# Attention scores and weighted sums as plain fp32 matmuls on half arrays, in double steps

## The reference, cut to what matters

```python
q, k, v = x @ Wq, x @ Wk, x @ Wv          # H = 16 heads, HKV = 4 key heads, D = 64
q, k = rope(q), rope(k)
scores = einsum('bkgqd,bkpd->bkgqp', q, k) * D ** -0.5
scores = where(causal, scores, -1e30)
out = einsum('bkgqp,bkpd->bkgqd', softmax(scores), v) @ Wo
```

## Time and profile before

| | |
|---|---|
| Median of 3 runs | 4915.38 us (4910.9 to 4915.8) |
| Span of the profiled execution | 4914.1 us |
| Its granted TensorE clock, mean | 0.959 |
| Attention's loop, about | 1770 to 3575 us of the span |

### The profile page before, as it was taken

The page is one execution under the profiler, slowest core; times in us unless marked ns, Lnnn a source line. Parts: engine busy times, 40 slices in busy tenths (PEclk is TensorE's granted clock), DMA queues, the critical chain, the costliest instruction groups (busy, mean ns, idle before and its releaser), DMA issues. The chain is left out here.

```text
span 4914.1 us, 82249 instructions
## 1 busy us (share of the span) xinstructions
PE 4375.7 (89%) x20280; PEld 3077.8 (63%) x20311; DVE 3433.2 (70%) x7334; ACT 2814.4 (57%) x6629; POOL 1757.2 (36%) x1411
## 2 busy tenths in 40 slices
PE   7888888789999979999999999999966549999996
PEld 3333333356666568888888888888855437777775
DVE  7999999934434878888888888888844443333336
ACT  7777777522221068888888888888833224444441
POOL 5989989700100021212121221212135553333330
PEclk8999999999999989999999999999987769999999
DMA  1000000021102530202112021202044425554548
GB/s 44 13 13 13 13 27 9 9 87 57 47 17 82 178 102 26 53 26 52 42 44 53 26 52 28 58 26 53 26 155 143 143 97 155 155 157 152 157 138 344
DMA packets 305965, 377.40 MB, mean 77 GB/s; under 512 B 123200, under 2 KB 236608, under 8 KB 300240
## 3 DMA queue, kind: packets, MB, share of 16 engines
q1 hardware_dynamic: 232784, 257.37, 17.3%
q0 software_dynamic: 26112, 73.44, 4.2%
q10 hardware_dynamic: 46944, 45.16, 3.4%
HBM read 223.07 MB, written 152.76 MB: 76 GB/s over the span
## 5 line engine op out<-in xcount | busy, mean ns | idle before, releaser
L1739 DVE TENSOR_TENSOR probsT<-ps_t,probsT 128x512 fp32r<-128x512 f32 (+3 forms) x1280 | 779.5, 609 | 137.8 <-ACT probsT L1679 116.2
L1679 ACT ACTIVATE probsT<-ps_t 128x512 fp32r<-128x512 f32 (+3 forms) x1280 | 686.6, 536 | 256.1 <-PE ps_t L1527 231.3
L1671 ACT ACTIVATE probs<-ps_s,negm 128x512 f32<-128x512 f32 (+3 forms) x1297 | 812.5, 627 | 28.1 <-DVE negm L1732 27.1
L1539 PE MATMUL ps_o<-probsT,vbuf 128*128 128x512 f32 (+3 forms) x2560 | 815.8, 402 | 6.8 <-ACT folding L1685 6.3
L1514 PE MATMUL ps_s<-kbuf,qbuf 128*128 (+1 forms) x2602 | 768.7, 380 | 57.8 <-ACT probs L1671 31.5
L1719 DVE TENSOR_REDUCE pmax<-ps_s 128x1 f32<-128x512 f32 (+3 forms) x1301 | 777.6, 600 | 47.3 <-PE ps_s L1514 23.0
L1527 PE MATMUL ps_t<-idn,probs 128*128 128x128 f32 x4352 | 694.8, 275 | 13.8 <-DVE probsT L1739 13.8
L527 POOL TENSOR_TENSOR dBx<-u,b_all 128x1024 f32<-128x1024 f32 x255 | 612.4, 2414 | 96.5 <-DVE h L623 66.8
L1527 PEld LDWEIGHTS ps_t<-idn,probs 128*128 128x128 f32 x4352 | 517.3, 141 | 135.3 <-DVE probsT L1739 40.9
L1514 PEld LDWEIGHTS ps_s<-kbuf,qbuf 128*128 128x128 f32 x2602 | 445.3, 189 | 177.9 <-issue 63.9
L1622 POOL CAST qbuf<-room_a 128x512 fp32r<-128x512 f32 x132 | 83.1, 630 | 1264.6 <-DMA room_a<-q_scr 754.1
(11 more groups left out here) (275 smaller groups left out, 6982.7 us busy)
## 6 DMA issues: line engine op xcount, KB each, us to landing
room_b<-xs ACTq DMA_DIRECT2D x294, 136.0 KB
room_a<-q_scr SPq DMA_DIRECT2D x528, 64.0 KB
room_c<-y SPq DMA_DIRECT2D x32, 1024.0 KB, 8.2
room_a<-W_guT SPq DMA_DIRECT2D x64, 384.0 KB
q_scr<-rot SPq DMA_DIRECT2D x64, 256.0 KB, 2.9
attn<-ostage SPq DMA_DIRECT2D x128, 128.0 KB
at<-attn SPq DMA_DIRECT2D x32, 512.0 KB
room_a<-W_downT SPq DMA_DIRECT2D x64, 192.0 KB
```

Source lines behind the costliest of these rows:

```text
L1539: last = nc.tensor.matmul(ps_o[:, lo:], vbuf[:, kb, :, :], probsT[:, g % SLOTS, part, lo:], start=kb == 0 and part == 0, stop=kb == BAND * ...
L1671: nc.scalar.activation(probs[:, k, at:at + n, :], ps_s[:, u % RING, 0:n * P], ACT.Exp, bias=negm[:, tile, :], accum_out=sums[:, s, j, c:c ...
L1679: nc.scalar.activation(probsT[:, g % SLOTS, 0, lo:], ps_t[:, t % 2, lo:], ACT.Copy).then_inc(high_t.sem, 1)
L1739: nc.vector.tensor_tensor(probsT[:, g % SLOTS, 1, lo:], ps_t[:, t % 2, lo:], probsT[:, g % SLOTS, 0, lo:].bitcast(F32), ALU.subtract).then ...
```

## The change

The split in high and low parts goes. Scores become one plain fp32 matmul over 64 rows; even and odd chunks use the lower and the upper 64 rows of the array (`rows`), where `qbuf` and `kbuf` hold the same data twice. Weighted sums become one plain fp32 matmul with 64 columns: even key blocks write the lower, odd ones the upper 64 rows of `ps_o`, and the fold adds them as before. The mask is added by two bf16 matmuls over 64 rows each. The turned groups are copied once, by ACT for even and by DVE for odd groups. `kbuf` is one buffer instead of two and is rewritten by quarters between two groups of heads, and `vbuf` comes straight from the staging buffer. TensorE's loop takes two steps at a time.

```diff
-    SLOTS = 4
+    SLOTS = 5
     LEAD = STEPS
     AHEAD = LEAD - BAND
-    LAG = 2
     LATE = STEPS - 2
...
+    def by_act(g):
+        return g % 2 == 0
...
+        def taken(eng, hx, t):
+            if ACT_TAKES[t + 1] > ACT_TAKES[t]:
+                eng.wait_ge(act_out.sem, act_out.at(hx, ACT_TAKES[t + 1]))
+            else:
+                eng.wait_ge(dve_out.sem, dve_out.at(hx, DVE_TAKES[t + 1]))
+        def bank_free(eng, hx, t):
+            if t >= 2:
+                taken(eng, hx, t - 2)
+            else:
+                taken(eng, hx - 1, NU * TURNS + t - 2)
...
-            def scores(hx, kslot, k, v):
+            def scores(hx, k, v):
                 s, j, c = CHUNKS[k][v]
                 u = k * STEPS + v
                 w = blocks(s, j, c) * P
+                rows = slice(HD * (u % 2), HD * (u % 2 + 1))
                 pe.wait_ge(exp_done.sem, exp_done.at(hx, u - RING + 1))
-                for part in range(2):
-                    last = nc.tensor.matmul(ps_s[:, u % RING, 0:w], qbuf[:, BAND * s + j, :],
-                                            kbuf[:, bass.ds(kslot, 1), part, c * CW:c * CW + w],
-                                            start=part == 0, stop=part == 1 and c < s)
+                last = nc.tensor.matmul(ps_s[:, u % RING, 0:w], qbuf[rows, BAND * s + j, :],
+                                        kbuf[rows, c * CW:c * CW + w], start=True, stop=c < s)
                 if c == s:
-                    last = nc.tensor.matmul(ps_s[:, u % RING, w - P:w], idn_r[:, :], mask_r[:, :], start=False, stop=True)
+                    for part in range(2):
+                        last = nc.tensor.matmul(ps_s[:, u % RING, w - P:w], halves_b[rows, part, :], mask_b[rows, part, :],
+                                                start=False, stop=part == 1)
                 last.then_inc(s_done.sem, 1)
             def turn(hx, k, g):
                 s, kb = GROUPS[k][g]
                 t = use(k, g)
                 pe.wait_ge(exp_done.sem, exp_done.at(hx, band_end(k, s)))
-                pe.wait_ge(t_out.sem, t_out.at(hx, t - 1))
+                bank_free(pe, hx, t)
                 for j in range(max(0, kb - BAND * s), BAND):
                     last = nc.tensor.transpose(ps_t[:, t % 2, j * P:(j + 1) * P], probs[:, k, place(k, s, j, kb), :], idn[:, :])
                 last.then_inc(t_done.sem, 1)
...
             def weigh(hx, group, k, g):
                 s, kb = GROUPS[k][g]
                 lo = max(0, kb - BAND * s) * P
-                pe.wait_ge(t_out.sem, t_out.at(hx, use(k, g) + 1))
+                rows = slice(HD * (kb % 2), HD * (kb % 2 + 1))
+                taken(pe, hx, use(k, g))
                 if kb == 0:
                     pe.wait_ge(o_ev.sem, o_ev.at(hx, 2 * k + (s == UNITS[k][1])))
                 if kb % BAND == 0:
                     pe.wait_ge(v_set.sem, v_set.at(group, V_ORDER.index(kb // BAND) + 1))
-                for part in range(2):
-                    last = nc.tensor.matmul(ps_o[:, lo:], vbuf[:, kb, :, :],
-                                            probsT[:, g % SLOTS, part, lo:],
-                                            start=kb == 0 and part == 0, stop=kb == BAND * s + BAND - 1 and part == 1)
-                last.then_inc(pv_done.sem, 1)
+                if kb == 1 and lo:
+                    nc.tensor.matmul(ps_o[rows, 0:lo], nothing[:, :], probsT[:, g % SLOTS, lo:2 * lo], start=True, stop=False)
+                nc.tensor.matmul(ps_o[rows, lo:], vbuf[:, kb, :], probsT[:, g % SLOTS, lo:],
+                                 start=kb == 0 or kb == 1 and not lo, stop=kb >= BAND * s + BAND - 2).then_inc(pv_done.sem, 1)
...
             with pe.Fori(0, NHEADS) as hx:
                 group = pe.snap(hx // GROUP)
-                slot = pe.snap(group % 2)
-                slot_next = pe.snap(((hx + 1) // GROUP) % 2)
+                group_next = pe.snap((hx + 1) // GROUP)
                 for k in range(NU):
                     def next_scores(v):
                         heads, unit, number = chunk(k, v, LEAD)
                         if number == 0 and unit == 0:
                             pe.wait_ge(q_ready.sem, q_ready.at(hx + 1, 2))
-                            pe.wait_ge(k_ready.sem, (hx + 1) // GROUP + 1)
                         elif number == 0:
                             pe.wait_ge(q_ready.sem, q_ready.at(hx + heads, 4))
-                        scores(hx + heads, slot_next if heads else slot, unit, number)
-                    for v in range(STEPS):
-                        if 0 < v < LATE:
-                            next_scores(v)
+                        if heads and unit == 0 and number < BANDS:
+                            pe.wait_ge(k_ready.sem, k_ready.at(group_next, K_ORDER.index(number) + 1))
+                        scores(hx + heads, unit, number)
+                    for v in range(0, STEPS, 2):
                         turn(hx, k, v)
-                        if v >= LAG:
-                            weigh(hx, group, k, v - LAG)
                         if v == FOLD[k]:
                             fold(hx, k, 0)
+                        turn(hx, k, v + 1)
+                        if v:
+                            weigh(hx, group, k, v - 2)
+                            weigh(hx, group, k, v - 1)
+                        next_scores(v + 1)
+                        next_scores(v + 2)
                     weigh(hx, group, k, STEPS - 2)
-                    next_scores(LATE)
                     weigh(hx, group, k, STEPS - 1)
-                    for v in range(LATE + 1, STEPS + 1):
-                        next_scores(v)
                     fold(hx, k, 1)
...
-            def keys(g):
...
+            def set_keys(g, c):
+                nc.gpsimd.tensor_copy(kbuf[:, c * CW:(c + 1) * CW], kstage[:, c * CW:(c + 1) * CW]).then_inc(k_ready.sem, 1)
             def queries(hx, n):
-                j, low = QUEUE[n], slice(HD, P)
-                tiles = slice(BAND * j, BAND * (j + 1))
-                after(q_ld[j].sem, q_ld[j].at(hx))
-                nc.gpsimd.tensor_copy(qbuf[:, tiles, :], qstage[:, tiles, :]).then_inc(high_q.sem, 1)
-                after(high_q.sem, high_q.at(hx, n + 1))
-                nc.gpsimd.tensor_tensor(qbuf[low, tiles, :], qstage[low, tiles, :], qbuf[low, tiles, :].bitcast(F32),
-                                        ALU.subtract).then_inc(q_ready.sem, 1)
-                after(q_ready.sem, q_ready.at(hx, n + 1))
+                tiles = slice(BAND * QUEUE[n], BAND * (QUEUE[n] + 1))
+                after(q_ld[QUEUE[n]].sem, q_ld[QUEUE[n]].at(hx))
+                nc.gpsimd.tensor_copy(qbuf[:, tiles, :], qstage[:, tiles, :]).then_inc(q_ready.sem, 1)
             def set_values(g, n):
                 b = slice(BAND * V_ORDER[n], BAND * (V_ORDER[n] + 1))
-                nc.gpsimd.tensor_copy(vbuf[:, b, :, :], vnext[:, b, :, :].bitcast(F32)).then_inc(v_set.sem, 1)
+                nc.gpsimd.tensor_copy(vbuf[:, b, :], vstage[:, b, :]).then_inc(v_set.sem, 1)
...
+                with pool.Fori(0, GROUP - 1) as j4:
                     head_queries(pool.snap(g * GROUP + j4))
+                head = pool.snap(g * GROUP + GROUP - 1)
+                after(s_done.sem, s_done.at(head, STEPS))
+                for n in range(2):
+                    queries(head + 1, n)
+                after(k_ld.sem, k_ld.at(g + 1))
+                for c in K_ORDER:
+                    after(s_done.sem, s_done.at(head, K_USED[c]))
+                    set_keys(g + 1, c)
+                for n in range(2, BANDS):
+                    queries(head + 1, n)
...
...
-                        high(hx, k, v)
+                        if by_act(v):
+                            take_turned(hx, k, v)
...
-            def low(hx, k, g):
+            def take_turned(hx, k, g):
                 s, kb = GROUPS[k][g]
                 t, lo = use(k, g), max(0, kb - BAND * s) * P
-                dve.wait_ge(high_t.sem, high_t.at(hx, k * STEPS + g + 1))
-                nc.vector.tensor_tensor(probsT[:, g % SLOTS, 1, lo:], ps_t[:, t % 2, lo:],
-                                        probsT[:, g % SLOTS, 0, lo:].bitcast(F32), ALU.subtract).then_inc(t_out.sem, 1)
+                dve.wait_ge(t_done.sem, t_done.at(hx, k * STEPS + g + 1))
+                dve.wait_ge(pv_done.sem, pv_done.at(hx, k * STEPS + g - SLOTS + 1))
+                nc.vector.tensor_copy(probsT[:, g % SLOTS, lo:], ps_t[:, t % 2, lo:]).then_inc(dve_out.sem, 1)
```

More of the change, by code:

```diff
@@ L1341, in attention @@
     RING = 5
-    SLOTS = 4
+    SLOTS = 5
     LEAD = STEPS
     AHEAD = LEAD - BAND
-    LAG = 2
     LATE = STEPS - 2
+    K_USED = [max(k * STEPS + v + 1 for k in range(NU) for v, (s, j, chunk_no) in enumerate(CHUNKS[k]) if chunk_no == c) for c in range(BANDS)]
+    K_ORDER = sorted(range(BANDS), key=lambda c: K_USED[c])
     V_ORDER = sorted(range(BANDS), key=lambda b: max(k * STEPS + g for k in range(NU) for g, (s, kb) in enumerate(GROUPS[k]) if kb // BAND == b))
```

(52 more changed lines are left out.)

59 lines of the change are left out of this document (22 added, 37 removed).

## The result

The changed kernel takes 5686.15 us (median of 4 runs, 5682.56 to 5688.06) against 4915.59 for the kernel before beside it: ratio 1.157, 95% interval 1.155 to 1.159. It is 771 us slower. The forecast said slower, 5890 us, range 5330 to 6220. So direction and range held, but two of the steps behind the number were wrong, in opposite directions.

A forecast was written before the change was run, and what follows sets the result against it. The prediction took TensorE to bound the attention stage. Per head 15.7 + 12.0 + 1.6 + 0.3 + 1.7 - 0.8 = +30.5 us, times 32 is +976, on 4914 gives 5890 us; range 5330 to 6220.

The forecast's parts named there:

- Overlap: Scores and weighted sums on half arrays: a pair takes three periods, the halves overlapping only in part; +15.7 us per head.
- B-high stands behind A-low: TensorE's queue for a pair of half-array matmuls: program order holds B's first record back, so 1.29 us against 0.94.
- first rival: TensorE's half-array matmuls: halves overlap fully, changes of shape still cost; +14.2 us per head, about 5370 us; chance 0.27.
- Changes of shape: TensorE switching between full array, column halves and row halves: 60 per head at 0.20 us, +12.0 us per head.
- Masks: Masked score chunks, 16 per head: one fp32r matmul becomes two bf16 on 64 rows, 0.10 each, +1.6 us per head.
- Folds: End of a unit: the fold waits uncovered for ACT's copy, the next second turn for the normalising; +1.7 us per head.
- Relief: DVE, ACT and POOL lose copies and low parts: only TensorE's wait for ACT's exponentials goes, -0.8 us per head.
- None of it stands on the path: Work taken off DVE, ACT and POOL: it doesn't set the time, except TensorE's 0.8 us per head wait for exponentials.
- the period of 0.43 inside a pair: Sign for the forecast in score pairs: second record and partner's first start within some ns, the next 0.43 us later.
- four starts within two periods: Sign in a pair's records on TensorE that the partial overlap was wrong and the halves overlap.
- 0.09 stops: Sign for the forecast on TensorE: weight loads start 0.09 us after the previous matmul's columns ended, three times per double step.
- wrong altogether: Sign against the whole forecast: TensorE idle for ACT or for POOL's keys by more than 2 us per head.

The follow-up runs named there:

- e7: Kernel before the change, with DVE's low part of the turned groups cut to 16 columns: 4901.97 us, ratio 0.9975 to the kernel before.
- e9: As e2, but scores and weighted sums each two fp32r matmuls over the full array, the second with zeros: ratio 1.005 to the kernel before, head 56.98 us.
- e4: As e2, but score and mask matmuls take all 128 rows, the upper 64 rows of the queries zero: 5349.98 us, ratio 1.109 to the kernel before.
- e1: Changed kernel, with DVE's copy of a turned group ahead of the peak of the same step: 5212.82 us, ratio 1.081 to the kernel before.
- e2: As e1, with all four weighs of a unit's last double step ahead of its two score chunks: 5147.30 us, ratio 1.067 to the kernel before.

## Why the prediction was right, and where it was wrong

The reading of the kernel before held: TensorE bounds the stage, which e7 confirms against DVE, and all else follows from its queue. The forecast's time was 204 us too high. Step by step, per head, where +30.5 was forecast and +23.9 measured:

1. *Overlap: wrong.* The step that failed is "B-high stands behind A-low". The forecast gave +15.7; the halves overlap fully where both are ready, and by e9 the matmuls cost no more than before. The row that the first rival had on its side, L277 begun before its predecessor's columns had ended, could not settle it, since its two matmuls share rows of the array (112 and 128 of them). So no row of before spoke of two halves, and I took program order for a rule across them. That order does not hold across the halves. In the trace a pair of 256 and 128 columns starts its records at 0.00 (256), 0.01 (128), 0.17 (128) and 0.27 (256). The one at 0.17 is the fourth in the program, and it starts before the second, at 0.27. The rule of the Trainium skill that I had leaned on ("TensorE: Matmul & The Clock Gate", The mechanism: matmuls keep program order in start and in end) differs from this trace, and the measurement decides: here order holds within a part of the array only. The Trainium skill's "TensorEngine Tiling (Array Packing)", Key Properties (the parts operate independently), agrees with it.

2. *Changes of shape: right, mis-sized by a fifth.* 60 at 0.20 were forecast, +12.0. Measured are 0.14 to 0.19, by the gaps 20 x 0.143 + 20 x 0.194 + 20 x 0.15 = 9.7; by runs it is 0.15 each (e4) and 0.16 (e9). The 16-row shape of the first stage gave the stop (0.09) but its weight load has 128 columns, where the sums have 64.

3. *Masks: not measured by themselves.* e9, which has the second mask matmul too, lies 0.6 above before with all that it has, where +1.6 was forecast for the masks alone.

4. *Folds: right in kind, short in size.* +1.7 forecast. Idle before the folds is 2.9 in the changed kernel, of which 1.2 is DVE's late copy, so 1.7 was its own part (e1 shows 1.7 left). e2 won 1.94 with it, one change per unit included.

5. *Relief: wrong.* The step that failed is "None of it stands on the path". I took -0.8 and measured +12.0 (e1; 15.1 at the turns, less 3.1 that came back as late score pairs), since I had counted DVE's load and not its order. The change moved the scores to the end of a double step and left DVE's peak ahead of its copy. What is queued behind a waiting instruction I had worked out for the folds and for the keys, but not for this peak. It could be seen by laying DVE's loop beside TensorE's new one.

So the measured sum is 9.7 for the changes, 12.0 for DVE's order, 1.9 for the folds, and the 0.3 that is left for all the rest: 23.9. The forecast's +15.7 for a cost that is not there stood in for the +12.0 that I had overlooked. That two errors nearly cancelled is luck, and the range held the result for the wrong reason in part: the first rival (full overlap, 5370) described the matmuls and is off by the 12.0 x 32 = 383 us of DVE's order, less 9.7 against 12.0 for the changes. Of what was to show the forecast, the head of 85 to 89 us with TensorE over 90% busy and the period of 0.43 inside a pair failed, and the four starts within two periods, its own sign of full overlap, are what came. The 0.09 stops, three per double step, DVE and ACT under 60% and the wait for ACT's folding copy came true. Its sign for "wrong altogether" named idle time for ACT or POOL; the 10.3 us per head were for DVE, which no sign named.

One thing stays open: how much of the score pairs' lateness another order on ACT and DVE would win back. By the estimate under e2 it is 4 us per head at most, and the change would still be slower than before.

## What to carry to other kernels

Matmuls on different halves of the array ran at the same time at full rate, even with two plain fp32 records each, but only where the second was ready when the first began; and every change between full, row and column shape cost 0.14 to 0.19 us here; so count the changes per unit of work first, and use halves only where long runs of one shape can be made. When an engine's work is moved to the end of a longer step, walk through each other engine's program in order and ask what stands behind the instruction that now waits longest: an engine that is 47% busy cost half of this loss. A high busy share of TensorE hides a pair whose halves don't overlap: compare the starts of the records. Relief of an engine that doesn't bound the kernel is worth the bounding engine's idle time at most, which the rows show beforehand (1.6 us per head here, of which e7 won 0.4).

## What was not expected of the hardware

- Records of the two halves start 0.01 us apart although each plain fp32 matmul is two records, and a later matmul of one half starts before an earlier one of the other.
- The stop at a change of shape is 0.090 to 0.092 us in all directions, from 16 rows as from 64 rows or 64 columns; the rest is the exposed weight load, 0.05 for the sums' 64 columns, 0.10 for the scores' 128 and 0.055 for the turns.
